# Merged row maxima, a bank of its own for their transposes, score masks in 32x32 tiles, and a reordered prologue

## The reference, cut to what matters

```
# layer 0: causal attention, 16 heads of width 8; keys and values come from ctx_1024
q, k, v = proj(layernorm(x)), proj(ctx), proj(ctx)
scores = where(j <= i, q k^T / sqrt(8), -inf);  attn = softmax(scores);  x = x + tanh(g) * (attn v) Wo
# layer 0: feed-forward with ternary weights and 8-bit activations
scale = 1 / clip(mean(|w|), 1e-5);  wq = clip(round(w * scale), -1, 1) / scale
x = x + tanh(g) * bitlinear(silu(bitlinear(x)) * bitlinear(x))
# layer 1: attention over 8 gathered keys per head, then 16 experts (2 chosen) with a shared one
```

## Time and profile before

| | |
|---|---|
| median of three runs | 186.11 us |
| the profiled execution's own time | 185.73 us |
| span of its records | 184.0 us |
| TensorE matmul busy | 162.1 us, 88% |
| VectorE busy | 129.0 us, 70% |
| ScalarE busy | 80.8 us, 44% |
| GpSimd busy | 55.8 us, 30% |
| first maxima of the attention start | 16.60 us |
| last maxima pair starts | 71.46 us |
| mean granted TensorE clock | 0.998 |

### The profile page before, as it was taken

One profiled execution on the slowest core, in us unless ns is written; L12 is line 12 of the kernel. 1 busy time (PEld: TensorE's weight loads), 2 busy tenths in 40 slices (PEclk: granted clock), 3 DMA queues, 4 the chain that ended last, 5 costly groups with the idle time before them and its releaser, 6 DMA issues.

```text
span 184.0 us, 3882 instructions
## 1 busy us (share of the span) xinstructions
PE 162.1 (88%) x1488; PEld 102.3 (56%) x1496; DVE 129.0 (70%) x359; ACT 80.8 (44%) x146; POOL 55.8 (30%) x91
## 2 busy tenths in 40 slices
PE   0478999999999997898678789999999998999993
PEld 0134456754565554556555666746776755666673
DVE  0697447488888896869889689586939485754543
ACT  2122555654465464667485863255521233212120
POOL 8750832639768534407203102600002000000000
PEclk9999999999999999999999999999999999999999
DMA  5986000000000000000000000000000000100001
GB/s 161 403 275 262 0 4 2 4 4 2 5 0 4 0 4 4 2 0 4 0 0 0 0 4 0 0 2 4 2 0 0 4 0 0 57 0 0 5 0 57
DMA packets 1891, 5.84 MB, mean 32 GB/s; under 512 B 208, under 2 KB 592, under 8 KB 1744
## 3 DMA queue, kind: packets, MB, share of 16 engines
q1 hardware_dynamic: 1152, 4.01, 6.0%
q10 hardware_dynamic: 720, 1.57, 2.3%
HBM read 5.06 MB, written 0.52 MB: 30 GB/s over the span
## 4 chain that ended last, share of the span: by engine, by line
PE 67%; DVE 18%; ACT 7%; DMA 3%; issue 3%; POOL 1%; SPq 0%; DVEq 0%
PE bank L1303 10%; PE bank L1328 10%; PE bank L1306 9%; PE bank L1090 8%; DVE bank L714 5%; PE bank L1082 3%; DMA x_all<-in_x 3%; PE bank L1136 3%; PE bank L1139 2%; PE bank L1099 2%; PE bank L1316 2%; ACT ffn_work L501 2%; PE bank L1022 2%; ACT f_hqT L507 2%; PE bank L1209 2%
## 5 line engine op out<-in xcount | busy, mean ns | idle before, releaser
L714 DVE TENSOR_REDUCE bank<-bank 128x4 f32<-128x512 f32 x32 | 22.3, 696 | 14.1 <-PE bank L1090 13.0
L285 POOL TENSOR_SCALAR_AFFINE_SELECT pT<-pT 128x512 f32<-128x512 f32 x32 | 19.9, 645 | 25.8 <-ACT pT L430 25.7
L1328 PEld LDWEIGHTS bank<-ews,rest 128*128 128x128 f32 x160 | 20.6, 191 | 7.8 <-issue 7.7
L430 ACT ACTIVATE pT<-bank 128x512 f32<-128x512 f32 x32 | 17.4, 596 | 10.0 <-PE bank L1120 9.9
L601 ACT ACTIVATE full<-bank 128x512 f32<-128x512 f32 x20 | 11.9, 593 | 21.9 <-PE bank L1303 21.9
L1328 PE MATMUL bank<-ews,rest 128*128 128x128 f32 x160 | 21.0, 275 | 0.0
L1303 PE MATMUL bank<-nT,ews 128*128 128x512 f32 x40 | 20.6, 597 | 0.2
L962 DVE TENSOR_TENSOR xnT<-full,bank 128x512 f32<-128x512 f32 x20 | 13.6, 682 | 10.0 <-PE bank L1306 7.7
L1306 PE MATMUL bank<-nT,ews 128*128 128x512 f32 x40 | 20.4, 592 | 0.0
L1099 PE MATMUL bank<-qm,kT 32*128 32x512 f32 x64 | 18.0, 640 | 0.0
L1090 PE MATMUL bank<-km,qT 32*128 32x512 f32 x64 | 17.3, 664 | 0.0
(11 more groups left out here) (167 smaller groups left out, 294.7 us busy)
## 6 DMA issues: line engine op xcount, KB each, us to landing
ews<-in_ew SPq DMA_DIRECT2D x1, 1928.5 KB, 7.6
fws<-in_fw SPq DMA_DIRECT2D x1, 768.0 KB, 8.1
cT<-in_ctxT ACTq DMA_DIRECT2D x2, 256.0 KB, 5.3
x_all<-in_x SPq DMA_DIRECT2D x2, 256.0 KB, 4.6
lws<-in_lw ACTq DMA_DIRECT2D x1, 449.0 KB, 8.3
sels<-in_sel ACTq DMA_DIRECT2D x1, 320.0 KB, 8.6
a<-in_aw ACTq DMA_DIRECT2D x1, 256.0 KB, 5.0
out_x<-x_all SPq DMA_DIRECT2D x1, 256.0 KB, 2.0
```

The costliest lines, as they stand in the source:

```text
L285: nc.gpsimd.affine_select(out=probs, in_=probs, compare_op=ALU.is_ge, fill=0.0, base=0, pattern=[[0, HG], [1, S]], channel_multiplier=-1). ...
L430: nc.scalar.activation(pT[:, j, :], bank[j][:, :], ACT.Exp, scale=SCALE).then_inc(sm["a_exp"], 1)
L714: V.tensor_reduce(group_max(j // 2)[:, j % 2, :], bank[j][:, :].rearrange("p (h k) -> p h k", h=4), AX.X, ALU.max).then_inc(sm["a_mx"], 1)
L1328: last = mm(bank[t][:, b * D:(b + 1) * D], e_h[:, u, b * S:(b + 1) * S], expert(c)[2], start=(c == 0 and (b == 0 or s == 1 and b == 2)), s ...
```

## The change: what it does

- **Maxima.** PSUM tensors are declared as four pairs of banks, and `top(n, p)` is one reduction over 128x1024 in place of two over 128x512. `split_max(n, 0)` follows it at once, ahead of `residual(n-2)`.
- **Transposed maxima** of elements 4 to 7 go to bank 4, without a wait for the residual.
- **Masks.** For each pair of banks, eight matmuls with 32x32 tiles take the place of two with 128x128. Bank 2p gets tiles on the diagonal of the array from `maskb`, bank 2p+1 tiles one row strip further on from a second mask, `maskt`, that GpSimd makes.
- **Dummy matmuls** (`keep_busy`) on a constant tile: 28 before the first load is waited for, 10 after `k_proj(0)`, 4 after `x_transposes(0)`.
- **Prologue order.** VectorE computes the second half's statistics after the first half's normalization and `km`, and normalizes the second half in the loop; ScalarE takes over two of four first `qm` copies and the sum of absolute weights (in three pieces). The second half's transposes, queries, values, the weight mean and the two layer-1 projections each move back by a half step or more.

```
+            V.memset(idle[:, :], 1.0).then_inc(sm["idle_ok"], 1)      # VectorE, first
+            pe.wait_ge(sm["idle_ok"], 1)
+            keep_busy(0, 28)                                          # [128x128] x [128x256] bf16 each
             pe.wait_ge(sm["ld_a1"], 16)
...
+            nc.gpsimd.memset(maskt[:, :], 0.0).then_inc(sm["ident_ok"], 1)
-            pool.wait_ge(sm["ident_ok"], 2)
+            pool.wait_ge(sm["ident_ok"], 3)
...
+            nc.gpsimd.affine_select(out=maskt[:, :], in_=maskt[:, :], compare_op=ALU.is_ge, fill=MASKED, base=-32, ...)
+            pool.wait_ge(sm["ident_ok"], 6)
+            nc.gpsimd.memset(maskt[0:32, :], 0.0).then_inc(sm["ident_ok"], 1)
+            pool.wait_ge(sm["ident_ok"], 7)
+            nc.gpsimd.affine_select(out=maskt[0:32, :], in_=maskt[0:32, :], compare_op=ALU.is_ge, fill=MASKED, base=96, ...)
+            pool.wait_ge(sm["ident_ok"], 8)
...
             def score_masks(n, p):
-                for j in (2 * p, 2 * p + 1):
+                for u, rows in enumerate((maskb, maskt)):
+                    j = 2 * p + u
                     if n:
                         pe.wait_ge(sm["a_exp"], 4 * (n - 1) + j + 1)
-                    mm(bank[j][:, :], identb[:, :], maskb[:, :].unsqueeze(1).to_broadcast([128, 4, S]),
-                       start=True, stop=False)
+                    for g in range(HG):
+                        of = strip((g + u) % HG)
+                        mm(bank[j][strip(g), :], identb[of, of], rows[of, :].unsqueeze(1).to_broadcast([32, 4, S]),
+                           start=True, stop=False, skip_group_check=True)
...
-            def top(n, j):
-                dve.wait_ge(sm["a_S"], 4 * n + j + 1)
-                if j % 2:
-                    dve.wait_ge(sm["a_mx"], 4 * n + j)
-                V.tensor_reduce(group_max(j // 2)[:, j % 2, :], bank[j][:, :]..., AX.X, ALU.max)
+            def top(n, p):
+                dve.wait_ge(sm["a_S"], 4 * n + 2 * p + 2)
+                V.tensor_reduce(bank[2 * p][:, 0:2 * HG], banks[p][:, :].rearrange("p (h k) -> p h k", h=2 * HG), AX.X, ALU.max)
...
+        def maxima_bank(n):
+            return bank[4 if n >= HALF else 6 + n % 2]
...
             def max_rows(n, p):
                 pe.wait_ge(sm["a_mid"], 2 * n + p + 1)
-                if n == 1 and p == 0:
-                    pe.wait_ge(sm["w_mean"], 1)
-                elif n >= 2 and p == 0:
+                if n == HALF and p == 0:
+                    pe.wait_ge(sm["proj_out"], J_RAW + 1)
+                elif 2 <= n < HALF and p == 0:
                     pe.wait_ge(sm["a_res"], n - 1)
...
# VectorE's prologue
+            input_stats(0)
             normalize_half(0)
             k_masked(0)
-            normalize_half(1)
-            dve.wait_ge(sm["ld_f"], 16)
-            V.tensor_reduce(fabs[:, :], fws[:, :].rearrange("p (m n) -> p m n", m=3), AX.X, ALU.add, apply_absolute_value=True)
-            for v in range(HG):
-                q_masked(0, v)
+            input_stats(1)
+            q_masked(0, 0)
+            q_masked(0, 1)
...
# VectorE's loop
             for n in range(B):
                 top(n, 0)
+                split_max(n, 0)
                 if n >= 2:
...                 # the wait for x_bo
                     residual(n - 2)
-                top(n, 1)
-                split_max(n, 0)
-                if n >= 2:
                     layer_stats(n - 2, (n - 2) // HALF)
-                if n == 3:
+                if n == 2:
+                    weight_scales()
+                elif n == 3:
                     q_masked(1, 1)
-                elif n == 4:
                     q_masked(1, 3)
...
-                top(n, 2)
-                top(n, 3)
+                top(n, 1)
                 split_max(n, 1)
                 if n:
                     heads_out(n - 1)
                 if n == 0:
-                    weight_scales()
+                    normalize_half(1)
...
# ScalarE: first_queries(2), first_queries(3) after q_copy(0); in the loop (second half of the batch)
#   n=0: k_copy(1), weights_abs(0);  n=1: xT_copy(1), weights_abs(1), weights_abs(2), then q_copy(1)
#   n=2: v_copy(1), then layer1_copy(0);  n=3: layer1_copy(1)
+            def weights_abs(m):
+                act.wait_ge(sm["ld_f"], 16)
+                nc.scalar.activation(fq32[:, bass.ts(m, INNER)], fws[:, bass.ts(m, INNER)], ACT.Abs, accum_out=fabs[:, m:m + 1])
...
# TensorE
             k_proj(0)
+            keep_busy(0, 10)
             x_transposes(0)
+            keep_busy(0, 4)
             q_proj(0)
-            pe.wait_ge(sm["ident_ok"], 4)
+            pe.wait_ge(sm["ident_ok"], 8)
...
             v_proj(0)
-            weight_sums()
...
             k_proj(1)
-            x_transposes(1)
...                 # in the loop, after the heads
# first half step:  before n=1 q_proj(1), n=2 layer1_proj(0)
#                   after  n=1 x_transposes(1), n=2 v_proj(1) and weight_sums(), n=3 layer1_proj(1)
# second half step: before n=1 v_proj(1), n=2 layer1_proj(1);  after n=1 q_proj(1), n=2 layer1_proj(0)
```

More of the change, by code:

```diff
@@ L60, in sem, with __init__, __getitem__ @@
             return es.enter_context(nc.semaphore(name))
-        bank = [es.enter_context(nc.psum_tensor(f"bank{i}", [128, 512], F32)) for i in range(8)]
+        banks = [es.enter_context(nc.psum_tensor(f"banks{i}", [128, 2 * 512], F32)) for i in range(4)]
+        class Bank:
+            def __init__(self, i):
+                self.pair, self.first = banks[i // 2], 512 * (i % 2)
+            def __getitem__(self, key):
+                rows, cols = key
+                stop = 512 if cols.stop is None else cols.stop
+                return self.pair[rows, self.first + (cols.start or 0):self.first + stop]
+        bank = [Bank(i) for i in range(8)]
         x_all = sb("x_all", [128, B * D])
@@ L305, in _ @@
                     bias_into_x0(0)
+                elif n == 1:
+                    bias_into_x0(1)
                 elif n == 3:
@@ L422, in max_copy @@
                 rows = slice(64 * p, 64 * p + 64)
-                nc.scalar.activation(mT[rows, :], bank[6 + n % 2][rows, 3 * S:4 * S], ACT.Copy)\
+                nc.scalar.activation(mT[rows, :], maxima_bank(n)[rows, 3 * S:4 * S], ACT.Copy)\
                     .then_inc(sm["a_mTs"], 1)
@@ L434, in _ @@
             q_copy(0)
+            act.wait_ge(sm["proj_out"], J_Q[0] + 1)
+            first_queries(2)
+            first_queries(3)
             v_copy(0)
@@ L638, in normalize, with input_stats @@
                                        ALU.subtract, ALU.mult)
-            for s in range(2):
+            def input_stats(s):
                 dve.wait_ge(sm[f"ld_x{s}"], 16)
@@ L685, in weight_scales @@
                 dve.wait_ge(sm["w_sum"], 1)
-                V.tensor_scalar(fmean[:, :], bank[7][:, 0:3], 1.0 / (INNER * D), None, ALU.mult).then_inc(sm["w_mean"], 1)
+                V.tensor_scalar(fmean[:, :], bank[4][:, 0:3], 1.0 / (INNER * D), None, ALU.mult).then_inc(sm["w_mean"], 1)
                 dve.wait_ge(sm["w_mean"], 1)
@@ L999, in _, with keep_busy @@
             mm = nc.tensor.matmul
+            def keep_busy(t, count):
+                for _ in range(count):
+                    mm(bank[t][:, 0:2 * S], idle[:, 0:128], idle[:, :], start=True, stop=True)
             def strip(j):
@@ L1041, in weight_sums @@
                 pe.wait_ge(sm["const_ok"], 3)
-                pe.wait_ge(sm["w_abs"], 1)
-                mm(bank[7][:, 0:3], ones_sq[:, :], fabs[:, :], start=True, stop=True).then_inc(sm["w_sum"], 1)
+                pe.wait_ge(sm["w_abs"], 3)
+                pe.wait_ge(sm["proj_out"], J_Q[1] + 1)
+                mm(bank[4][:, 0:3], ones_sq[:, :], fabs[:, :], start=True, stop=True).then_inc(sm["w_sum"], 1)
             def layer1_proj(w):
@@ L1090, in scores @@
                     mm(bank[j][:, :], qT[strip(j), n * S:(n + 1) * S], km[strip(j), n, :, :].rearrange("p v t -> p (v t)"),
-                       start=False, stop=True).then_inc(sm["a_S"], 1)
+                       start=False, stop=True, skip_group_check=True).then_inc(sm["a_S"], 1)
             def transposed_scores(n, p):
@@ L1104, in max_rows @@
                 pe.wait_ge(sm["a_mid"], 2 * n + p + 1)
[L1105 to L1107 removed]
+                if n == HALF and p == 0:
+                    pe.wait_ge(sm["proj_out"], J_RAW + 1)
+                elif 2 <= n < HALF and p == 0:
                     pe.wait_ge(sm["a_res"], n - 1)
                 rows = slice(64 * p, 64 * p + 64)
[L1110 removed]
+                mm(maxima_bank(n)[rows, 3 * S:4 * S], mxs[:, p, :, :].rearrange("p g r -> p (g r)"), identb[:, :],
                    start=True, stop=True).then_inc(sm["a_mT"], 1)
@@ L1170, in _ @@
                 if n == 1:
-                    q_proj(1)
+                    x_transposes(1)
                 elif n == 2:
-                    layer1_proj(0)
+                    v_proj(1)
+                    weight_sums()
```

(6 more changed lines are left out.)

39 lines of the change are left out of this document (26 added, 13 removed).

## The result

The changed kernel takes **181.17 us** (four runs, 181.16 to 181.19); the forecast was 181.1. The kernel before took 186.4 in the same comparison (185.67 to 187.43). The ratio is 0.9716, 95% interval 0.9667 to 0.9764: faster. The profiled execution went from 185.73 to 181.17 us, 4.56 less; forecast 4.6.

The account below looks back on a forecast made before the run. It took the loop as bound by TensorE's own list, and by the chain through VectorE's maxima in six stretches. Prologue 2.9 + maxima 1.6 + masks 0.35 - jobs 0.6 + copy 0.4 = 4.6 us off 185.73: 181.1, range 178.6 to 184.4.

Parts of the forecast that it names:

- Clock: Prologue: dummy matmuls put keys, transposes and queries at TensorE's higher level; q_proj(0) 1.06 us instead of 2.08, first maxima at 14.4.
- The rival of a late clock: Prologue: the clock does not rise in time and 2.6 us forecast from the higher level are lost; 185.0 us, chance 0.08.
- GpSimd's additions: Prologue: memsets, selects and waits put ahead of rstd_of(0, 0) on GpSimd take 1.35 us, bounds 0.6 to 2.1.
- Merged maxima: Loop: one reduction of 1024 elements takes 1.22 us against 1.50 for a pair; 1.6 us gained.
- The six stretches: Parts of the loop and its end where the chain of waits runs through VectorE's maxima; 0.27 us gained in each.
- Masks: score_masks in the loop: eight tiles, issued 27 ns apart, take 0.40 us against 0.43; 0.05 in seven half steps, 0.35 gained.
- masks all at once: Rival: mask tiles all start together, 0.15 us more in seven half steps, and GpSimd's prologue is 0.7 shorter; 179.3 us, chance 0.11.
- A page's rule: Masks: weight loads run ahead only where row groups differ, so a pair takes about 0.6 us; total gain near 2.5.
- One by one: Rival, every score_masks: the eight tiles run one after another, 1.72 us instead of 0.43; 202 us, chance 0.13.
- Moved jobs: Loop's TensorE list gets x_transposes(1), 0.44 us, and the weight sum, 0.15, in TensorE-bound half steps; 0.6 lost.
- The copy done earlier: q_masked(1, 3) is done an element earlier, so element 4's transposed scores no longer start late; 0.4 us gained.
- Order of the residual: Loop: removing the wait for the residual costs and brings nothing, as the residual was done before the split.

## Why the prediction was right, step by step

The number was right to 0.1 us, and that is partly luck: the masks gave 0.36 more than forecast and the merged maxima 0.3 less.

- **Clock.** Right: keys, transposes and queries run at the higher level, the first maxima start at 14.39 (14.4). The rival of a late clock did not occur in the changed kernel's runs. A clock that falls again before `q_proj(0)` lies near: four of 24 runs with the same work up to there had a mean of 0.991.
- **GpSimd's additions.** Put at 1.35 us; measured 1.18 (rstd starts at 7.61 instead of 6.43). Right in kind too: moved away, they give 1.21.
- **Merged maxima.** 1.22 us forecast, 1.23 measured. The six stretches gave 1.32 instead of 1.6. The second half step of element 3 gave 0.04 instead of 0.27. VectorE's and GpSimd's timelines there, in the changed kernel and then in the kernel before:

```profile
42.27 1.52 POOL L321 TENSOR_TENSOR kb<-full,lws 128x512 f32<-128x512 f32 x1
...
42.96 1.11 DVE L711 TENSOR_SCALAR qm<-qT,a 128x512 f32<-128x512 f32 x1
...
45.21 1.51 POOL L294 TENSOR_TENSOR kb<-full,lws 128x512 f32<-128x512 f32 x1
...
46.12 0.88 DVE L664 TENSOR_SCALAR qm<-qT,a 128x512 f32<-128x512 f32 x1
```

  In both kernels the query copy begins while GpSimd's product runs and ends 0.28 us after it (44.07 and 43.79; 47.00 and 46.72). It begins 0.26 earlier in the half step than before, but the product ends only 0.03 earlier, so the copy takes 1.11 instead of 0.88. The half step's gain went there.
- **Masks.** The term that was mis-sized: 0.35 forecast, 0.71 measured. The floor of 27 ns for each issue was wrong for these tiles: all eight start within 0.03 us at 22.16 and make a piece of 0.34, where I took 0.40. The rival "masks all at once" (0.11) had this part right and was too large elsewhere. And the term acts in other places than I said: 0.09 to 0.21 in the five half steps with a projection job, nothing in elements 5 and 6, where the exp comes last.
- **A page's rule.** The loads and matmuls of the second four tiles start 0.01 us after those of the first four, though all row groups are in use. By the rule on weight loads (the Trainium skill, TensorE: Matmul & The Clock Gate, Part 3) they would have waited; the trace disagrees. With the same four tiles for both banks the loads did not wait either; the matmuls did, by 0.23 us.
- **One by one** (0.13). Did not happen: distinct row strips wrote one bank at once, on 32 partitions each. The rule of the Trainium skill, TensorEngine Tiling (Array Packing), Gotcha 1, taken by whole banks, does not hold for these rows at 22.16.
- **Moved jobs.** 0.6 lost was forecast. The five half steps from element 1 to the second of element 3 went from 19.85 to 19.75; with the masks' 0.71 taken off, the jobs cost 0.61. No run moves the jobs alone, so this is a difference and not a measurement.
- **The copy done earlier.** 0.4 forecast; the second half step of element 4 went from 3.43 to 3.06.
- **Order of the residual, put at nothing.** It is worth 0.25, in elements 4 and 7. The forecast had no term for it and counted those half steps under the maxima.

## What to carry to other kernels

Before work is moved "into an idle engine", look at what runs beside it. Here a VectorE instruction that began during a long GpSimd one ended just after it (4.01 us for 1.11 beside the memset), and the gap of 3.2 us that this opened on TensorE cost 1.7 us with the clock kept and up to 3.8 without. Of equal pieces in a chain, ask for each place what its second half waits for: the same masks were worth 0.2 us in one half step and nothing in the next. The reordering of the prologue brought nothing to the first maxima without the matmuls that keep the engine busy through it.

## What the runs showed of the hardware that was not expected

- Eight 32x32 tiles at distinct places started within 0.03 us of each other and ran at once, four row strips into one bank. With the same four tiles for both banks the weight loads still started together, the second four matmuls 0.23 us later, and the piece grew from 0.34 to 0.54 us.
- A VectorE normalization of 1.11 us took 4.01 beside a 3.51 us GpSimd memset that had begun before it, and a clip of 0.39 took 1.61 beside a product of 1.52. Where the clip began 0.02 us ahead, it took 0.39 and the product 1.77.
- After idle stretches of 1.55 us (8.4 to 9.95, in one run of several), 2.3 us and 3.2 us, the granted clock fell from 1.00 to 0.50. The first time the next projection took 2.06 us instead of 1.12. One of the four runs with the 3.2 us stretch in its list had a mean clock of 1.000, but left no trace.
